# A causal attention step and a routed layer on one core: dense groups behind the last pair, transposes a pair ahead, x1 of the seventh step taken sooner

## The chip, the cores and the metric

The kernel runs on one core of a Trainium2 chip, as one launch. The core has TensorE (matmuls), VectorE, ScalarE, GpSimd and SyncE, which run their own instruction lists beside each other and wait for each other through semaphores. The metric is device time in microseconds (us). Traces are of one profiled execution; times in it count from the span's start.

## The reference

Two sequences of 2048 rows with 256 columns pass through two layers. The first: rows are normalized, three small networks (matmul, exact gelu, matmul) make q, k and v, masked scores without softmax weigh v, and the result, normalized again, is added to x. The second: each row is normalized and multiplied by one of 8 weight matrices, chosen by its position in the sequence.

```python
q, k, v = mlp_q(ln(x)), mlp_k(ln(x)), mlp_v(ln(x))     # gelu(x @ W1 + b1) @ W2 + b2
scores = einsum('bid,bjd->bij', q, k) / scale * tril
x = x + ln(einsum('bij,bjd->bid', scores, v)) * ln_w + ln_b
idx = argmax(pe @ sign(tile_sigs).T, axis=-1)          # one of 8 per position
y_all = einsum('bsd,tod->bsto', ln(x), W) + b
x = x + take_along_axis(y_all, idx, axis=2)
```

## The kernel before

**Numbers.** Float32 values are split in a rounded part and a rest, and a product is three matmuls (rounded by rounded, rounded by rest, rest by rounded; `mm3`, L493). Making an operand therefore takes two steps: ScalarE casts from PSUM ("rounded"), and VectorE subtracts the cast from the original ("rest").

**Attention.** The 4096 rows are taken in 8 steps of 512 rows, each of 4 chunks of 128. A state (k transposed times v) carries earlier steps. In the last step (s = LAST = 7) the chunks are handled by `last_scores`, `last_state` and `last_out`: output c of that step is its chunk c's attention result. GpSimd takes the powers for the two normalizations (`rstd_out`, `rstd_x1`), VectorE makes x1, the first layer's result (`x1_final`, `x1_stats`, `x1_var`).

**Sorting.** Rows of x1 go out by `rows_sorted`: an indirect DMA from GpSimd, one per chunk, which scatters them by their matrix into a buffer in HBM (`sorted_rows`), so that each slot of 128 rows needs one matrix. There are 37 slots; SyncE loads them back (`load_slot`). The last two chunks of the last step are not sorted ("dense", "unsorted"): all 8 matrices are applied to them and a one-hot factor picks the right result. Slots from 17 on may hold rows of step s = 6, the seventh, so their loads wait for its scatters; slots from 21 on wait for those of the last step's first two chunks.

**Pairs.** Slot 0 goes alone; the other 36 are 18 pairs, m = 0 to 17. A pair passes through: `pair_norm` (ScalarE, two instructions), `pair_transposes` (TensorE, 4 transposes), `pair_rounded` (ScalarE), `pair_rest` (VectorE), `pair_products` (TensorE, 12 matmuls), `pair_out` (VectorE adds the result to the rows) and two scatters to the output by GpSimd (`slots`). The 256 dense rows pass through the same places between pairs 11 and 12 (`PAIRS` stands for them). For that, `place` shifts the later pairs:

```python
        def place(m):
            return m if m < LATER else LATER if m == PAIRS else m + 1
```

`pair_transposes` takes a place and `pair_products` a pair; LATER is 12, so `pair_transposes(13)` turns the rows of pair 12. Products go to one bank, w_ps, for m < 8 and in turn to three from there; the transposes of places 5 to 7 share one bank (ring 1), and from 8 on there are three.

**Dense groups.** `dense_products(e, g)` is one of 8 groups of 6 matmuls with 512 columns (chunk e of the two, matrices 2g and 2g + 1), with two PSUM banks in turn; `dense_out` reads each with two VectorE instructions. When all four groups of a chunk are in, SyncE sends the chunk out.

**Order.** There is no scheduler: each engine's order is written out by hand in the blocks for the engines, and an engine that waits holds everything behind it in its list.

Of the kernel before, what the change touches and what calls it, by code (L numbers as in the profile page):

```python
# [37 lines left out]
CH = GT // P  # L38
PER = T // GT
STEPS = NB * PER  # L40
LAST = STEPS - 1
NT = 8
# [10 lines left out]
SLOTS = NB * NJ - DENSE + NT - 1  # L53
# [3 lines left out]
AMID, INNER, MIDDLE, LATER = 1, 5, 8, 12  # L57
# [15 lines left out]
def mk_seq_kernel(nc, x, w1, w2, bias_cols, rows3, sigs2, ffn_w, ffn_b, pe, out):  # L73
# [5 lines left out]
    with ExitStack() as ctx:  # L79
# [408 lines left out]
        def _(te):  # L488
# [193 lines left out]
            def dense_products(e, g):  # L682

                i = NT // 2 * e + g
                if i == 0:
                    te.wait_ge(xb_lo, AMID + LATER + 1)
                if i < 2:
                    te.wait_ge(o_cen, CH * STEPS)
                else:
                    te.wait_ge(dense_done, 2 * (i - 1))  # L690
                mm3(o_ps[i % 2][:, :], [[pair_xb(PAIRS, a)[:, cols(2 * e + k)] for a in range(2)] for k in range(KC)],
                    [[wf[:, a, k, 2 * g * C:2 * g * C + 2 * C] for a in range(2)] for k in range(KC)]
                    ).then_inc(dense_ps, 1)
# [17 lines left out]
            def last_state(c):  # L711

                if c == 0:
                    te.wait_ge(s_lo, splits_before(LAST, 0))
                i = CH * LAST + c
                if c < 2:
                    te.wait_ge(o_sq, i - 1)
                elif c == 3:
                    te.wait_ge(o_cen, i - 2)
                mm3(last_o[c][:, 0:C], [q_chunk(k, c) for k in range(KC)],  # L720
                    [[state[:, a, k * C:k * C + C] for a in range(2)] for k in range(KC)], stop=False)

            def last_out(c):
                if c == 0:
                    te.wait_ge(v_lo, 2 * STEPS)
                    te.wait_ge(off_lo, 3)
                    te.wait_ge(sc_lo, STEPS)
                pairs = []
                for j in range(c):
                    at = off_at[j] + (c - j - 1) * P  # L730
                    pairs.append([sc_off[:, a, at:at + P] for a in range(2)])
                pairs.append([scT[:, a, cols(c)] for a in range(2)])
                mm3(last_o[c][:, 0:C], pairs, [[vtok[:, a, j, :] for a in range(2)] for j in range(c + 1)], start=False
                    ).then_inc(o_ready, 1)
# [113 lines left out]
            pair_transposes(5)  # L848
            last_out(0)
            last_out(1)  # L850
            last_state(2)
            last_out(2)
            pair_products(5)
            last_state(3)
            last_out(3)
            pair_transposes(6)
            pair_products(6)
            pair_transposes(7)
            pair_products(7)
            pair_transposes(8)  # L860
            pair_products(8)
            pair_transposes(9)
            pair_products(9)
            pair_transposes(10)
            pair_transposes(11)
# [2 lines left out]
            pair_products(11)  # L868
            for m in range(LATER, PAIRS):
                pair_transposes(m + 1)  # L870
                dense_products((m - LATER) // 4, (m - LATER) % 4)
                pair_products(m)
            for i in range(PAIRS - LATER, NT):
                dense_products(i // 4, i % 4)

        @block.scalar
        def _(act):
# [218 lines left out]
            k_rounded(LAST, 0)  # L1096
            k_rounded(LAST, 1)
            pair_norm(4)
            v_rounded(LAST, 0)
            pair_rounded(4)  # L1100
            v_rounded(LAST, 1)
            last_rounded(1)
            last_rounded(0)
# [23 lines left out]
        def _(dve):  # L1127
# [447 lines left out]
            out_centred(s, 3)  # L1575
            pair_out(1)
            pair_rest(2)
            q_rest(LAST)
            pair_out(2)
            pair_rest(3)  # L1580
            x1_final(s, range(CH))
            k_rest(LAST, 0)
            x1_stats(s, range(CH))
            k_rest(LAST, 1)
            x1_var(s, range(CH))
            state_rest(s, 3)
            pair_out(3)
            v_biased(LAST, 0)
            pair_rest(4)
            v_biased(LAST, 1)  # L1590

            last_masked(1)
# [12 lines left out]
            out_centred(LAST, 1)  # L1605
            last_aggregates((0, 1))
            last_centred((0, 1))
            out_centred(LAST, 2)
            x1_final(LAST, (0, 1))
            x1_stats(LAST, (0, 1))  # L1610
            x1_var(LAST, (0, 1))
            pair_out(5)
            pair_rest(6)
            out_centred(LAST, 3)
            last_aggregates((2, 3))
            last_centred((2, 3))
# [14 lines left out]
            pair_out(11)  # L1631
            for m in range(LATER, PAIRS):
                pair_rest(m)
                g = m - LATER
                dense_out(g // 4, g % 4 * 2)
                dense_out(g // 4, g % 4 * 2 + 1)
                pair_out(m)
            for g in range(PAIRS - LATER, NT):
                dense_out(g // 4, g % 4 * 2)
                dense_out(g // 4, g % 4 * 2 + 1)  # L1640

        @block.gpsimd
        def _(pool):
# [167 lines left out]
            rstd_out(s)  # L1811
            slots((3, 4, 5, 6))
            rstd_x1(s)
            rows_sorted(s, (0, 1))
            slots((7, 8))
            pool.wait_ge(o_ready, CH * LAST + 2)
            rows_sorted(s, (2, 3))
            rstd_out(LAST, (0, 1))
            slots((9, 10))
            rstd_x1(LAST, (0, 1))  # L1820
            rows_sorted(LAST, (0, 1))
            rstd_out(LAST, (2, 3))
            slots((11, 12))
            rstd_x1(LAST, (2, 3))
            slots(range(13, SLOTS))


def position_table(seq, dim):
# [50 lines left out]
```

## Time and profile before

| | us |
|---|---|
| median of 3 runs | 312.46 |
| the runs | 312.4, 312.46, 314.71 |
| profiled execution, its time | 314.41 |
| profiled execution, its span | 312.7 |
| TensorE busy in the span | 288.1 |
| VectorE, ScalarE, GpSimd busy | 237.3, 188.3, 176.7 |

The span runs from the first to the last instruction in the profile; the execution's time is a little longer than it. The busy times are sums over the whole span. Mean granted TensorE clock over the span is 0.992 of full speed.

### The profile page before, as it was taken

The page shows a single profiled execution, that of the slowest core. Times are in us where ns is not written, and L with a number is a line of the kernel's source. Part 1 is how long each engine was busy: PE and PEld are TensorE (multiplying, and loading weights), DVE is VectorE, ACT ScalarE, POOL GpSimd, SP SyncE. Part 2 cuts the span into 40 slices and gives each one's busy share as a digit, 9 for nine tenths or more (in the row PEclk, how much of TensorE's full clock was granted, in tenths as well). Part 3 has the DMA queues.
Part 4 walks back from the last instruction along what each step waited for, and adds up shares of the span by engine and source line. Part 5 has one row for each costly group of instructions (what it writes and reads, how often), then busy time and mean ns, then how long its engine had stood idle before and what let it go on. Part 6 is the DMA issues. An engine that isn't in the chain of part 4 may idle for free.

```text
span 312.7 us, 5456 instructions
## 1 busy us (share of the span) xinstructions
PE 288.1 (92%) x1806; PEld 253.4 (81%) x1806; DVE 237.3 (76%) x539; ACT 188.3 (60%) x380; POOL 176.7 (57%) x238
## 2 busy tenths in 40 slices
PE   8999998998999999999999999999999985579991
PEld 6789887997888889889788989898988884477870
DVE  5769788899879978967995896788558778246661
ACT  2565775776656876786678658669674434264410
POOL 6881532360685568475737545584564578745452
PEclk9999999999999999999999999999999999979998
DMA  7909950011022120211031000260223234922110
GB/s 223 230 17 334 350 175 28 0 45 58 0 74 67 36 71 2 68 69 39 6 131 53 18 2 2 72 198 2 88 86 123 71 100 149 313 85 68 48 42 17
DMA packets 24209, 27.83 MB, mean 89 GB/s; under 512 B 4659, under 2 KB 22068, under 8 KB 24118
## 3 DMA queue, kind: packets, MB, share of 16 engines
q1 hardware_dynamic: 15910, 13.68, 14.7%
q0 software_dynamic: 3296, 8.64, 8.0%
q10 hardware_dynamic: 4976, 5.16, 4.9%
q8 instruction: 15, 0.25, 0.3%
q14 instruction: 12, 0.10, 0.1%
HBM read 13.95 MB, written 14.44 MB: 91 GB/s over the span
## 4 chain that ended last, share of the span: by engine, by line
PE 75%; DVE 13%; issue 5%; POOL 3%; ACT 2%; DVEq 0%; POOLq 0%; ACTq 0%
PE ring L493 40%; PE o_ps L493 11%; PE s_ps L493 6%; PE w_ps L493 3%; PE ring L502 2%; PE ring L521 2%; PE sc_ps L606 2%; DVE xres L1245 1%; POOL sorted_rows L1715 1%; PE sc_ps L604 1%; PE ring L764 1%; PE sc_ps L764 1%; DVE xnT L1166 1%; DVE st L1252 1%; DVE state L1210 1%
## 5 line engine op out<-in xcount | busy, mean ns | idle before, releaser
L493 PE MATMUL ring<-xnT,w_sp 128*128 128x512 f32 x288 | 73.5, 399 | 3.6 <-DVE hT L1171 1.7
L493 PEld LDWEIGHTS ring<-xnT,w_sp 128*128 128x128 f32 x288 | 51.9, 189 | 15.9 <-issue 3.3
L892 ACT ACTIVATE ring<-ring,b_cols 128x512 f32<-128x512 f32 x48 | 31.7, 660 | 27.1 <-PE ring L493 25.7
L493 PE MATMUL ring<-hT,w_sp 128*128 128x512 f32 x192 | 46.7, 397 | 0.2 <-DVE hT L1171 0.2
L1171 DVE TENSOR_TENSOR hT<-ring,hT 128x512 fp32r<-128x512 f32 x48 | 32.5, 681 | 13.8 <-ACT hT L895 12.2
L493 PEld LDWEIGHTS ring<-hT,w_sp 128*128 128x128 f32 x192 | 35.2, 188 | 8.8 <-DVE hT L1171 0.9
L1715 POOL DMA_INDIRECT sorted_rows<-xres,slot_i x30 | 31.3, 1042 | 12.3 <-issue 6.2
L1681 POOL TENSOR_TENSOR vtok<-v,vtok 128x512 fp32r<-128x512 f32 x14 | 18.0, 1286 | 25.0 <-ACT vtok L912 24.9
L1780 POOL DMA_INDIRECT out_dram<-slot_rows x22 | 21.8, 989 | 14.7 <-DVE slot_rows L1464 9.2
L895 ACT CAST hT<-ring 128x512 fp32r<-128x512 f32 x48 | 28.2, 587 | 1.5
L493 PE MATMUL s_ps<-vtok,ktok 128*128 128x256 f32 x168 | 24.8, 284 | 0.0
L1245 DVE SCALAR_TENSOR_TENSOR xres<-cen,rs,xres 128x256 f32<-128x256 f32 x32 | 23.7, 754 | 1.3 <-issue 1.0
L493 PEld LDWEIGHTS ring<-w_sp,hT 128*128 128x128 f32 x192 | 23.4, 188 | 0.7
L493 PE MATMUL ring<-w_sp,hT 128*128 128x256 f32 x192 | 23.9, 280 | 0.0
L493 PE MATMUL o_ps<-state,q_eye 128*128 128x256 f32 x116 | 23.2, 293 | 0.0
L1660 POOL TENSOR_SCALAR nm<-mv 128x4 f32<-128x4 f32 x7 | 1.6, 229 | 38.0 <-DVE mv L1160 38.0
L493 PEld LDWEIGHTS s_ps<-vtok,ktok 128*128 128x128 f32 x168 | 22.1, 191 | 0.0
L1674 POOL TENSOR_TENSOR xres<-xt,row_stage 128x1024 f32<-128x1024 f32 x8 | 22.0, 2752 | 0.0
L1780 POOL DMA_INDIRECT out_dram<-h x15 | 15.4, 1030 | 10.1 <-DVE h L1464 6.9
L1210 DVE TENSOR_TENSOR state<-s_ps,state 128x512 fp32r<-128x512 f32 x27 | 18.3, 678 | 2.1 <-ACT state L928 1.9
L945 ACT ACTIVATE xn<-xt,sh,rs 128x256 f32<-128x256 f32 x28 | 16.7, 598 | 4.9 <-POOL sh L1665 4.9
L493 PEld LDWEIGHTS o_ps<-state,q_eye 128*128 128x128 f32 x116 | 18.4, 190 | 1.5 <-issue 0.6
(241 smaller groups left out, 680.6 us busy)
## 6 DMA issues: line engine op xcount, KB each, us to landing
sorted_rows<-blank ACTq DMA_DIRECT2D x1, 5032.0 KB, 20.7
xt<-x SPq DMA_DIRECT2D x7, 512.0 KB, 3.5
slot_rows<-sorted_rows SPq DMA_DIRECT2D x22, 136.0 KB
w_stage<-tile_w SPq DMA_DIRECT2D x8, 256.0 KB, 3.2
h<-sorted_rows SPq DMA_DIRECT2D x15, 136.0 KB
xt<-x SPq DMA_DIRECT2D x2, 256.0 KB, 2.9
hT<-position_table POOLq DMA_DIRECT2D x1, 512.0 KB, 10.0
sorted_rows<-xres,slot_i POOLq DMA_INDIRECT x30
```

The lines of the kernel that those rows point to most:

```text
L493: last = te.matmul(o, lhs[k][a], rhs[k][c], start=start and k == 0 and i == 0, stop=stop and k == n - 1 and i == 2, skip_group_check=check)
L502: te.matmul(ring[2][:, :], warm_r[:, 0:P], warm_r[:, :], start=True, stop=True)
L892: nc.scalar.activation(full, ring[(2 + m) % 3][:, :], ACT.Gelu, bias=b1c[:, m // 2, m % 2:m % 2 + 1]).then_inc(gelu, 1)
L895: nc.scalar.copy(hT[:, m, 0, :], full).then_inc(h_hi, 1)
L945: last = nc.scalar.activation(xn[:, c, :], xt[s % 2][:, c, :], ACT.Identity, bias=sh1[:, c:c + 1], scale=rs1[:, c:c + 1])
L1171: nc.vector.tensor_tensor(hT[:, m, 1, :], ring[(2 + m) % 3][:, :], hT[:, m, 0, :].bitcast(F32), ALU.subtract).then_inc(h_lo_dve, 1)
L1210: nc.vector.tensor_tensor(state[:, 1, :], s_ps[:, :], state[:, 0, :].bitcast(F32), ALU.subtract).then_inc(s_lo, 1)
L1245: nc.vector.scalar_tensor_tensor(out=xres[s % XR][:, c, 0:C], in0=cen[:, c, :], scalar=rs2[:, c:c + 1], in1=xres[s % XR][:, c, 0:C], op0=A ...
L1674: nc.gpsimd.tensor_tensor(xres[s % XR][:, :, 0:C], xt[s % 2][:, :, :], lnb_row[:, :].unsqueeze(1).broadcast_to([P, CH, C]), ALU.add).then_ ...
L1681: nc.gpsimd.tensor_tensor(vtok[:, 1, 2 * j:2 * j + 2, :], v32[:, 2 * j:2 * j + 2, :], vtok[:, 0, 2 * j:2 * j + 2, :].bitcast(F32), ALU.sub ...
L1715: pool.indirect_dma_start(out=sorted_rows, out_offset=bass.IndirectOffsetOnAxis(ap=at, axis=0), in_=xres[s % XR][:, c, :], in_offset=None) ...
L1780: pool.indirect_dma_start(out=out_rows, out_offset=bass.IndirectOffsetOnAxis(ap=row_buf(n)[:, PLACE:PLACE + 1].bitcast(I32), axis=0), in_= ...
```

## The change

It moves work; nothing is computed differently. The matmuls are the same, and so are the DMAs.

- TensorE: the transposes of pairs 6 to 9 each stand one pair earlier, ahead of the products of the pair before. The transposes of pair 6 and the products of pair 5 stand ahead of state product and output 2 instead of behind them. In the loop over pairs 12 to 17 the dense group between transposes and products is gone; all 8 dense groups stand behind pair 17.
- ScalarE: the cast of pair 4 stands ahead of the first cast of v.
- VectorE: x1 of step s = 6 is made in two halves around q's rests, and its statistics and variance stand earlier; the rest of pair 4 stands ahead of both v additions. The addition of pair 5 and the rest of pair 6 stand ahead of x1 of the last step's chunks 0 and 1, and the statistics of output 2 behind it. The dense instructions stand behind pair 17.
- GpSimd: the four row scatters of step s = 6 go out in one piece, without a wait for output 1 of the last step; two more output scatters (slots 9 and 10) stand ahead of the first power of the last step, and the later slots move up accordingly.

```diff
@@ tensor
             last_out(0)
             last_out(1)
+            pair_transposes(6)
+            pair_products(5)
             last_state(2)
             last_out(2)
-            pair_products(5)
             last_state(3)
             last_out(3)
-            pair_transposes(6)
+            pair_transposes(7)
             pair_products(6)
-            pair_transposes(7)
+            pair_transposes(8)
             pair_products(7)
-            pair_transposes(8)
+            pair_transposes(9)
             pair_products(8)
-            pair_transposes(9)
             pair_products(9)
             pair_transposes(10)
             pair_transposes(11)
...
             for m in range(LATER, PAIRS):
                 pair_transposes(m + 1)
-                dense_products((m - LATER) // 4, (m - LATER) % 4)
                 pair_products(m)
-            for i in range(PAIRS - LATER, NT):
+            for i in range(NT):
                 dense_products(i // 4, i % 4)
@@ scalar
             pair_norm(4)
+            pair_rounded(4)
             v_rounded(LAST, 0)
-            pair_rounded(4)
@@ vector
             pair_rest(2)
-            q_rest(LAST)
+            x1_final(s, (0, 1))
+            q_rest(LAST, (0,))
+            x1_final(s, (2, 3))
+            q_rest(LAST, (1,))
             pair_out(2)
+            x1_stats(s, range(CH))
             pair_rest(3)
-            x1_final(s, range(CH))
+            x1_var(s, range(CH))
             k_rest(LAST, 0)
-            x1_stats(s, range(CH))
             k_rest(LAST, 1)
-            x1_var(s, range(CH))
             state_rest(s, 3)
             pair_out(3)
+            pair_rest(4)
             v_biased(LAST, 0)
-            pair_rest(4)
             v_biased(LAST, 1)
...
-            out_centred(LAST, 2)
+            pair_out(5)
+            pair_rest(6)
             x1_final(LAST, (0, 1))
             x1_stats(LAST, (0, 1))
             x1_var(LAST, (0, 1))
-            pair_out(5)
-            pair_rest(6)
+            out_centred(LAST, 2)
             out_centred(LAST, 3)
...
             for m in range(LATER, PAIRS):
                 pair_rest(m)
-                g = m - LATER
-                dense_out(g // 4, g % 4 * 2)
-                dense_out(g // 4, g % 4 * 2 + 1)
                 pair_out(m)
-            for g in range(PAIRS - LATER, NT):
+            for g in range(NT):
                 dense_out(g // 4, g % 4 * 2)
                 dense_out(g // 4, g % 4 * 2 + 1)
@@ gpsimd
             rstd_x1(s)
-            rows_sorted(s, (0, 1))
-            slots((7, 8))
-            pool.wait_ge(o_ready, CH * LAST + 2)
-            rows_sorted(s, (2, 3))
+            rows_sorted(s, range(CH))
+            pool.wait_ge(scores, CH * LAST + 2)
+            slots((7, 8, 9, 10))
             rstd_out(LAST, (0, 1))
-            slots((9, 10))
+            slots((11, 12))
```

On TensorE, in the turn of pair 17: the transposes (L764), then in before a dense group, then the first of the products (`ISA` rows set the address of the matrix).

```order
 L493 MATMUL s_ps<-wf,xnT 128x256 x2
 L764 MATMUL sc_ps<-ident,xn 128x128 x4
-L493 MATMUL o_ps<-wf,kT 128x512 x6
 L493 ISA
 L493 MATMUL ring<-wf,xnT 128x256
```

The group of 6 matmuls is taken out; the transposes and products of pair 17 stand directly behind each other. The end of TensorE's list:

```order
 L493 ISA
 L493 MATMUL ring<-wf,xnT 128x256 x2
-L493 MATMUL o_ps<-wf,kT 128x512 x12
+L493 MATMUL o_ps<-wf,kT 128x512 x48
 L79 UNCONDITIONAL_BRANCH
```

Behind pair 17 there were two dense groups (12 matmuls), and now there are eight (48).

On VectorE, where x1 of the last step's first two chunks is made (L1245), with its statistics (L1252) and variance (L1263), before:

```order
L1223 BN_STATS st<-s_ps 128x6 [waits o_ready]
L1245 SCALAR_TENSOR_TENSOR xres<-cen,rs,xres 128x256 [waits res_done,rstd2,o_cen]
L1245 SCALAR_TENSOR_TENSOR xres<-cen,rs,xres 128x256
L1252 BN_STATS st<-xres 128x6 [waits x1_made]
L1252 BN_STATS st<-xres 128x6
L1263 BN_AGGR mv<-st 128x2 [waits stat3,shift3]
L1263 BN_AGGR mv<-st 128x2
L1267 TENSOR_SCALAR nm<-mv 128x2 [waits aggr3]
L1268 TENSOR_SCALAR ve<-mv 128x2
L1464 TENSOR_TENSOR slot_rows<-w_ps,slot_rows 128x2x256 [waits y_ps]
L1456 TENSOR_TENSOR xb<-ring,xb 128x512 [waits xb_hi]
L1223 BN_STATS st<-o_ps 128x6 [waits o_ready]
```

and the same place changed (the lines are one lower there):

```order
L1463 TENSOR_TENSOR slot_rows<-w_ps,slot_rows 128x2x256 [waits y_ps]
L1455 TENSOR_TENSOR xb<-ring,xb 128x512 [waits xb_hi]
L1244 SCALAR_TENSOR_TENSOR xres<-cen,rs,xres 128x256 [waits res_done,rstd2,o_cen]
L1244 SCALAR_TENSOR_TENSOR xres<-cen,rs,xres 128x256
L1251 BN_STATS st<-xres 128x6 [waits x1_made]
L1251 BN_STATS st<-xres 128x6
L1262 BN_AGGR mv<-st 128x2 [waits stat3,shift3]
L1262 BN_AGGR mv<-st 128x2
L1266 TENSOR_SCALAR nm<-mv 128x2 [waits aggr3]
L1267 TENSOR_SCALAR ve<-mv 128x2
L1222 BN_STATS st<-s_ps 128x6 [waits o_ready]
L1222 BN_STATS st<-o_ps 128x6 [waits o_ready]
```

The addition of pair 5 and the rest of pair 6 (L1464 and L1456 in before) have moved ahead of x1, and the statistics of output 2 (`st<-s_ps`) behind it.

On GpSimd, from the row scatters of step s = 6 to the first power of the last step, before:

```order
L1715 DMA sorted_rows<-xres,slot_i 4736x272 [waits shift3]
L1715 DMA sorted_rows<-xres,slot_i 4736x272
L1780 DMA out_dram<-h 4096x256 [waits y_done] x2
L1715 DMA sorted_rows<-xres,slot_i 4736x272 [waits shift3,o_ready]
L1715 DMA sorted_rows<-xres,slot_i 4736x272
L1693 TENSOR_TENSOR ve<-mv,eps 128x2 [waits o_aggr]
L1695 TENSOR_TENSOR rs<-ve,half 128x2 [waits var2]
L1780 DMA out_dram<-h 4096x256 [waits y_done] x2
```

and changed (the lines are two lower there):

```order
L1713 DMA sorted_rows<-xres,slot_i 4736x272 [waits shift3]
L1713 DMA sorted_rows<-xres,slot_i 4736x272 x3
L1778 DMA out_dram<-h 4096x256 [waits y_done,scores]
L1778 DMA out_dram<-h 4096x256 [waits y_done] x3
L1691 TENSOR_TENSOR ve<-mv,eps 128x2 [waits o_aggr]
L1693 TENSOR_TENSOR rs<-ve,half 128x2 [waits var2]
L1778 DMA out_dram<-slot_rows 4096x256 [waits y_done] x2
```

The four row scatters stand together, their wait for output 1 (`o_ready`) is gone, and slots 9 and 10 stand ahead of the power.

## Rows read from the trace of the kernel before

**Rows 1.** The page: busy time, share of the span, instructions
```profile
PE 288.1 (92%) x1806; PEld 253.4 (81%) x1806; DVE 237.3 (76%) x539; ACT 188.3 (60%) x380; POOL 176.7 (57%) x238
```

**Rows 2.** Windows: busy us (instructions) in each stretch, clock, DMA share, GB/s
```profile
256.35:271.60 15.25, 9.14 (x70) 7.97 (x68) 9.71 (x27) 6.28 (x12) 12.03 (x16) 1.00 0.72 228
271.60:275.29 3.69, 0.00 (x0) 0.00 (x0) 0.98 (x2) 1.57 (x3) 2.90 (x3) 1.00 0.76 242
276.70:280.10 3.40, 3.40 (x18) 3.34 (x17) 1.98 (x3) 2.19 (x5) 0.54 (x1) 0.50 0.11 39
286.80:301.33 14.53, 14.21 (x89) 11.75 (x89) 9.22 (x17) 5.43 (x11) 7.49 (x9) 1.00 0.14 47
```

**Rows 3.** The chain that ended last: start us, us, what
```profile
297.71 1.70 PE s_ps L493 x12
299.41 0.44 PE sc_ps L764 x4
299.85 1.40 PE o_ps L493 x6
301.25 0.08 issue
...
303.04 2.82 PE o_ps L493 x12
```

**Rows 4.** Timeline of TensorE: start us, us, what, xcount [idle before <-releaser]
```profile
236.83 1.58 PE L493 MATMUL w_ps<-wf,xb 128*128 x12
...
243.72 0.50 PE L493 MATMUL sc_ps<-q_eye,kT 128*128 128x512 f32 x1 [0.46 <-DVE xb L1456]
...
258.43 1.69 PE L493 MATMUL w_ps<-wf,xb 128*128 x12 [1.48 <-DVE xb L1456]
259.96 0.60 PE L764 MATMUL ring<-ident,xn 128*128 128x128 f32 x4
262.04 1.70 PE L493 MATMUL w_ps<-wf,xb 128*128 x12 [1.48 <-DVE xb L1456]
...
265.84 1.70 PE L493 MATMUL ring<-wf,xnT 128*128 x12 [1.66 <-DVE xnT L1456]
...
271.00 0.60 PE L764 MATMUL ring<-ident,xn 128*128 128x128 f32 x4
```

**Rows 5.** Timeline of ScalarE
```profile
250.09 0.59 ACT L1013 CAST xb<-ring 128x512 fp32r<-128x512 f32 x1 [1.93 <-PE ring L764]
250.57 1.09 ACT L986 ACTIVATE xn<-slot_rows 128x255 f32<-128x255 f32 x2
...
260.59 0.58 ACT L1013 CAST xb<-ring 128x512 fp32r<-128x512 f32 x1 [2.04 <-PE ring L764]
...
273.67 0.58 ACT L1013 CAST xb<-ring 128x512 fp32r<-128x512 f32 x1 [4.08 <-remote]
```

**Rows 6.** Timeline of VectorE
```profile
254.75 0.88 DVE L1245 SCALAR_TENSOR_TENSOR xres<-cen,rs,xres 128x256 f32<-128x256 f32 x2 [1.04 <-issue]
...
262.18 0.88 DVE L1245 SCALAR_TENSOR_TENSOR xres<-cen,rs,xres 128x256 f32<-128x256 f32 x2 [0.28 <-POOL rs L1695]
...
264.42 0.68 DVE L1464 TENSOR_TENSOR slot_rows<-w_ps,slot_rows 128x512 f32<-128x512 f32 x1
265.02 0.68 DVE L1456 TENSOR_TENSOR xnT<-ring,xnT 128x512 fp32r<-128x512 f32 x1
267.58 0.69 DVE L1464 TENSOR_TENSOR slot_rows<-ring,slot_rows 128x512 f32<-128x512 f32 x1 [1.88 <-issue]
```

**Rows 7.** Timeline of GpSimd
```profile
251.40 0.96 POOL L1715 DMA_INDIRECT sorted_rows<-xres,slot_i  x1 [4.09 <-PE o_ps L493]
...
257.43 0.76 POOL L1704 TENSOR_TENSOR xres<-ve,half 128x2 f32<-128x2 f32 x1
...
261.36 0.72 POOL L1695 TENSOR_TENSOR rs<-ve,half 128x2 f32<-128x2 f32 x1
```

**Rows 8.** Timeline of SyncE's DMA queue
```profile
255.19 1.76 SPq L456 DMA_DIRECT2D slot_rows<-sorted_rows  x4
```

More of the change, by code:

```diff
@@ L1822, in _ @@
             rstd_out(LAST, (2, 3))
-            slots((11, 12))
+            slots((13, 14))
             rstd_x1(LAST, (2, 3))
-            slots(range(13, SLOTS))
+            slots(range(15, SLOTS))
 def position_table(seq, dim):
```

## The prediction

> **What bounds the kernel now.** I read the page first, then the end by stretches of time, then the chain of waits there, then each engine's timeline. The page says that TensorE is busy for 92% of the span and the others for 57 to 76% [rows 1]. That is an average. By stretches [rows 2], TensorE is busy from 256.35 to 271.60 us for 9.14 of 15.25 us; for the next 3.69 us it does nothing; from 286.80 to 301.33 us it is busy for 14.21 of 14.53 us. So two kinds of pair loop follow each other. In the first, TensorE waits in each turn; in the second, the wait is filled.
>
> The chain shows what fills it [rows 3]. One turn of the second loop is the products of a pair (1.70 us), the transposes of the next pair (0.44), one dense group (1.40) and a wait of 0.08: 3.62 us. The pair's other way, from the transposes through ScalarE's cast ("R" below) and VectorE's subtraction ("rest" below) to the products, runs beside the dense group and ends 0.08 us behind it. The first loop has no dense group, and its turn is as long: products start at 258.43, 262.04 and 265.84 us, 3.61 and 3.80 us apart, each after a wait of 1.48 to 1.66 us for VectorE [rows 4]. The turn there is the serial way itself: transposes to R 0.63 us (259.96 to 260.59), R to products 1.45 (to 262.04), products to the next transposes 1.53 (258.43 to 259.96), in sum 3.61 [rows 4, 5]. So a dense group costs TensorE nothing where it stands now.
>
> **The dense groups behind pair 17 (the largest term).** In before, six of the eight dense groups stand in the turns of pairs 12 to 17 and two behind pair 17. Changed, all eight stand behind it. The turns of pairs 12 to 17 still begin with the transposes of their own pair: behind LATER the place of pair m is m + 1, so `pair_transposes(m + 1)` turns the rows of pair m, and only the taken-out group stood between those transposes and the products that need them. So the turn keeps its serial length, 3.6 us as in [rows 4], and saves nothing. Behind pair 17 the six groups lie on the path in full: two of them back to back take 2.82 us of the chain [rows 3], 1.41 each, and 6 x 1.41 = **8.46 us**. VectorE doesn't stretch this: in the second loop it is busy for 9.22 of 14.53 us [rows 2], 2.30 a turn, and an addition and a rest of 0.69 each leave 0.92 for its two instructions of a group, less than 1.41, with two o_ps banks to go round. Bounds: if each turn shrank by the 0.08 us of waiting, 0.5 less; if the five whole turns came out like the slowest of the first loop, 3.80, 5 x 0.18 = 0.9 more. I take 8.46.
>
> **Transposes a pair ahead, pairs 6 to 9.** Here the change does put the next pair's transposes before the products, and R and the next rows' normalization run under them. What is left in a turn is products to VectorE's addition (265.84 to 267.58: 1.74), addition to rest (264.42 to 265.02: 0.60) and rest to products (265.02 to 265.84: 0.82) [rows 4, 6], since VectorE still takes the addition of pair m before the rest of pair m + 1. That is 3.16 us where 3.61 was, 0.45 a turn and not the whole wait of 1.48. Only pair 9 gets it clean: pair 8 is set by VectorE's statistics of the last step (next part), and from pair 10 on the order of the transposes is as before. Gain **0.45**.
>
> **VectorE and GpSimd ahead of pair 8.** I follow the changed order from where it first helps. TensorE waits 0.46 us at 243.72 for the rest of pair 4 [rows 4], whose R stood behind a v cast and whose rest stood behind a v addition. Both now go first, well before 243. TensorE goes on without the wait, so output 1, on which GpSimd's scatter at 251.40 waited in before [rows 7], is ready about 0.5 us sooner.
> The transposes of pair 6 now stand directly behind output 1. Their normalization comes from R of pair 5, 250.09 - 0.5, and ends 1.57 us later (250.09 to 251.66) [rows 5]: 251.2. TensorE waits some 0.6 us there, which the change adds; queued behind it on TensorE are the products of pair 5, outputs 2 and 3. VectorE waits for the first of these and takes outputs 2 and 3 later than before. Products of pair 5 then start at 251.5, and those of pair 6, with outputs 2 and 3 between, near 257.2 instead of 258.43.
> On VectorE the addition of pair 5 starts at 251.5 + 1.74 = 253.2, the rest of pair 6 at 253.8, the first two x1 chunks of the last step at 254.4 where they were at 254.75. From there to the end of their statistics and variance it is 2.3 us (262.18 to 264.42 and a little, for the same instructions) [rows 6]: 256.7 instead of 257.1. GpSimd took that variance only at 257.43, when its scatter before it was over [rows 7]. Now its two scatters there start with the addition of pair 5, 253.2 + 0.7, take 2 x 1.3 us and end at 256.5, so it takes the variance at 256.75, 0.7 us sooner, and with it the two row scatters and the power behind them (start 261.36). VectorE's last x1 chunks wait for exactly that power, by 0.28 us [rows 6]. So they, their statistics, the addition of pair 7, the rest of pair 8 and its products all come 0.7 us sooner: 265.84 becomes 265.1. That is **0.7 us** of gain. Bounds: 1.2 (TensorE's lead at pair 6 kept in full) and a loss of 0.6 (GpSimd a scatter of 1.3 us late).
>
> **x1 of the seventh step sooner.** Two additions of 0.44 us each (as at 254.75 [rows 6]) go in front of each half of q's rest, and statistics in front of the rest of pair 3, which comes some 0.7 us later, near 236.1. TensorE takes it at 236.83 [rows 4]; q's rest is first asked for later still. So this costs nothing while TensorE's queue covers it, and without that cover 0.7 us. GpSimd's four scatters of these rows go out together before 245 us; in before the last two waited for output 1 until 251.40 [rows 7]. SyncE's loads of slots 17 to 20, at 255.19 in before [rows 8], follow at about 246. But pair 8, their first user, was not waiting for them: it ran straight behind R of pair 7 (260.59) [rows 5]. I cost this at 0. The loads from slot 21 on hang on the last step's scatters, which come 0.7 us sooner; pair 10, their first user, comes 1.15 us sooner, behind work of some 4 us since they landed. GpSimd's scatters of a pair, 2 x 1.27 us, stay under the turn of 3.16 and cost nothing.
>
> **The sum.** -0.7 - 0.45 + 8.46 = **+7.3 us**. The profiled execution took 314.41 us for a span of 312.7; the median is 312.46. I take the difference as one event: the transposes of pair 10 start at 271.00 and R follows at 273.67, 2.0 us later than the usual 0.63 [rows 4, 5], with nothing of the program between. 314.41 - 2.0 = 312.4, the median. So the sum goes on the median: 312.46 + 7.3 = **319.8 us**. If the event comes in most executions of the changed kernel, 321.8. After the idle 3.69 us the granted clock is 0.50, the 1.2 GHz level, from 276.70 to 280.10, with TensorE busy all the while [rows 2]: that costs at most half of it, 1.7 us. I leave it where it is in both; without it in the changed kernel, 318.1.
>
> **The rivals.** (a) *The clock falls in the pair loop.* TensorE now rests some 1.5 us in each turn from 256 to 297 us, over 40 us where it was 15. Against it: through 15.25 us of the same rhythm the granted clock was 1.00 [rows 2]. For it: the fall at 276.70 came behind such turns and one longer pause. Price: at half the clock the products and transposes of a turn, 2.14 us, would take up to 2.1 more, 1.3 to 1.9 after what pipelining hides; 8 to 11 us in six turns: 328 to 331. Chance 7%. [...]
> (b) *The pair loop speeds up* (the case that is not slower). If the transposes of pairs 12 to 17 came a pair ahead of their products, a turn would be TensorE's own 1.70 + 0.44 and little else, 2.2 instead of 3.62: 6 x 1.42 = 8.5 back, and the result 311.3, within 1%. It decides from a turn of about 2.9 us down (8.46 - 1.15 - 3.1 = 4.2 us to win back in six turns, 0.7 each). Against it: the first loop, with the same order, turns in 3.61 [rows 4]. 3%.
> (c) *More is won in front.* SyncE's loads and GpSimd's scatters ran together up to 275 us at 228 to 242 GB/s [rows 2]. With four loads and two scatters moved ahead of that stretch, the late R at 273.67, the idle 3.69 us and the clock's fall could shrink in every execution. That gives up to 3 us: 317 to 318. 12%.
>
> **How the numbers follow.** Forecast 78%, (c) 12, (a) 7, (b) 3. Predicted 319.8. The range takes in the bounds of the loop (-0.5, +0.9), of the front (-0.5, +1.3), the event (+2.0) and most of (c): 317.5 to 323.0; outside lie (a), (b) and a part of (c). About 1%, 3 us, is what a measurement of this kernel can tell from no change. Slower by over 1%: 96%; within 1%: 3%; faster: 1%.
>
> **What would show it.** In the changed profile: turns of pairs 12 to 17 of 3.6 us, each with a wait of about 1.5 us for VectorE; eight dense groups in one run of some 11.3 us at the end; products of pair 9 some 3.2 us after pair 8's, and pair 8's at 265.1; the four scatters of step seven before 245 us and the load of slot 17 near 246; granted clock 1.00 through the loop. I am wrong if a turn of the late loop is under 3 us, if the clock falls inside it, or if pair 8 starts later than 265.8.

## The result, and the profile after

The changed kernel takes **318.8 us** (median of 4 runs, 316.95 to 320.04) beside 312.65 us for the kernel before on the same chip: ratio **1.0171, interval 1.0135 to 1.0208**. A second measurement on another chip (below) gave 318.85 beside 313.19, ratio 1.0151 [1.0117, 1.0185]. So it is slower, by 6.2 us in the first and 5.7 in the second, where 7.3 were forecast. The profiled execution took 316.95 us for a span of 315.2, at a mean granted clock of 0.994, and was the shortest of the four; the others had 0.973 to 0.983.

The page of the changed kernel: busy time, then TensorE's busy share and its granted clock in 40 equal slices of the span, in tenths:

```profile
PE 288.2 (91%) x1806; PEld 253.7 (80%) x1806; DVE 237.6 (75%) x539; ACT 189.0 (60%) x380; POOL 176.7 (56%) x238
...
PE   8999999998999999999999999999999984665695
...
PEclk9999999999999999999999999999999999899999
```

TensorE's row has the sixes of the pair loop, where it used to be full, and the nine of the dense groups behind it. The timeline of TensorE in the changed kernel (start us, us, what, then in brackets the idle time ahead and what ended it), from the first changed place to the end; it answers to [rows 4]:

```profile
236.20 1.58 PE L493 MATMUL w_ps<-wf,xb 128*128 x12
...
242.46 0.39 PE L493 MATMUL sc_ps<-q_eye,kT 128*128 128x512 f32 x1
...
250.34 0.66 PE L764 MATMUL ring<-ident,xn 128*128 128x128 f32 x4 [0.60 <-ACT xn L985]
250.76 1.69 PE L493 MATMUL w_ps<-wf,xb 128*128 x12
...
256.59 1.68 PE L493 MATMUL w_ps<-wf,xb 128*128 x12
...
264.85 1.70 PE L493 MATMUL ring<-wf,xnT 128*128 x12 [2.99 <-DVE xnT L1455]
268.01 1.71 PE L493 MATMUL w_ps<-wf,xnT 128*128 x12 [1.46 <-issue]
269.55 0.60 PE L764 MATMUL ring<-ident,xn 128*128 128x128 f32 x4
272.77 0.66 PE L764 MATMUL ring<-ident,xn 128*128 128x128 f32 x4 [2.62 <-ACT xn L985]
...
287.93 1.71 PE L493 MATMUL ring<-wf,xb 128*128 x12 [1.48 <-DVE xb L1455]
...
291.55 1.70 PE L493 MATMUL w_ps<-wf,xb 128*128 x12 [1.48 <-DVE xb L1455]
...
298.81 1.70 PE L493 MATMUL ring<-wf,xnT 128*128 x12 [1.48 <-DVE xnT L1455]
300.35 11.59 PE L493 MATMUL o_ps<-wf,kT 128*128 128x512 f32 x48
```

From pair 14 on the turns of the late loop are 3.62 us (287.93 to 291.55) with a wait of 1.48 in each (pair 13, ahead of them, waits 1.79), and the eight dense groups take 11.6 us in one run. Both are as forecast, and at first sight the sum of them explains the result. It doesn't: from the start of pair 17's products the changed kernel needs 315.2 - 298.8 = 16.4 us, and the kernel before needed 312.7 - 301.33 = 11.4 [rows 2]. That is 5.0 us more, not 8.46. Where the missing 3.5 us are shows in a view that the prediction did not open, GpSimd's timeline at the very end. The kernel before:

```profile
304.56 0.97 POOL L1780 DMA_INDIRECT out_dram<-h  x1 [1.38 <-DVE h L1464]
305.83 0.97 POOL L1780 DMA_INDIRECT out_dram<-h  x1 [0.30 <-issue]
```

and the changed one:

```profile
302.03 0.97 POOL L1778 DMA_INDIRECT out_dram<-h  x1 [1.37 <-DVE h L1463]
303.31 0.97 POOL L1778 DMA_INDIRECT out_dram<-h  x1 [0.30 <-issue]
```

In before, the span ends 6.9 us after GpSimd's last scatter began (305.83 to 312.7), and TensorE's last dense group was over by 305.9. SyncE's waits in the last microseconds of the kernel before (engine, line, what it waited for: us in total, times, longest):

```profile
SPq L79 <- PEq L79: 3.7, 1, 3.7
SPq L79 <- DMA out_dram<-xres: 0.7, 1, 0.7
SPq L485 <- DMA out_dram<-h: 0.6, 1, 0.6
```

and of the changed kernel:

```profile
SPq L79 <- DMA out_dram<-xres: 1.3, 1, 1.3
SPq L79 <- PEq L79: 0.2, 1, 0.2
```

Line 79 is the closing of the program, where the engines meet. In before, SyncE had seen the last scattered rows land (the wait at L485) and its own output too, and then stood there for 3.7 us; in the changed kernel for 0.2. The engine named is TensorE's queue, but TensorE had been done for long: the name only says that the one who came last is not seen. The experiments say who it was.

### The profile page after: what moved, and what is told of

Its sections match the earlier page's. It is cut to its first block, busy times and chain, and to the rows that moved or that the text cites. A ratio compares the mean times of both kernels' runs of the same rounds, so it can differ in the third digit from the quotient of the medians.

```text
span 315.2 us, 5456 instructions
## 1 busy us (share of the span) xinstructions
PE 288.2 (91%) x1806; PEld 253.7 (80%) x1806; DVE 237.6 (75%) x539; ACT 189.0 (60%) x380; POOL 176.7 (56%) x238
## 4 chain that ended last, share of the span: by engine, by line
PE 76%; DVE 11%; issue 6%; ACT 4%; POOL 1%; ACTq 0%; POOLq 0%; DVEq 0%
PE ring L493 41%; PE o_ps L493 11%; PE s_ps L493 6%; PE w_ps L493 3%; ACT xn L985 2%; PE ring L502 2%; PE ring L521 2%; PE sc_ps L606 2%; PE ring L764 1%; PE sc_ps L764 1%; PE sc_ps L604 1%; DVE xnT L1165 1%; DVE st L1151 1%; DVE xres L1244 1%; DVE xnT L1455 1%
```

## The experiments

All medians are device microseconds; the kernel before was run beside each: 313.01 us on the first chip (the first four kernels), 313.19 on the second (the next four), 313.16 on the third (the last four).

**1. Only the dense groups behind pair 17**, the rest as before.

```diff
             for m in range(LATER, PAIRS):
                 pair_transposes(m + 1)
-                dense_products((m - LATER) // 4, (m - LATER) % 4)
                 pair_products(m)
-            for i in range(PAIRS - LATER, NT):
+            for i in range(NT):
                 dense_products(i // 4, i % 4)
```

(and VectorE's two dense instructions of each group likewise)

> Only the dense groups are moved behind pair 17; all else as in the kernel before. My theory (the groups were hidden beside the serial way of a pair, and lie open behind pair 17): 6 x 1.41 = 8.5 us slower than before, 321.1; turns of pairs 12 to 17 of 3.6 us. Rival, the turn shrinks when the group is gone: 0 to 1 us slower. Rival, the granted clock falls in the loop in most executions: 1 to 3 us more, 322 to 324, and a mean clock near 0.975 in those runs.

Measured: 317.66 us, ratio 1.0159 [1.0126, 1.0193]: 4.7 us more than before, where the theory wanted 8.5. Its profiled execution had a granted clock of 1.00 throughout, turns of 3.62 us and 11.59 us of dense groups at the end. So the rhythm of TensorE is as forecast and the bill is 3.8 us short. The profiled span ends at 315.2, as the changed kernel's does.

**2. Only the front**: the changed kernel with the dense groups back in the loop, that is, the diff of run 1 taken the other way on the changed kernel.

> The changed kernel with the dense groups back in the turns of pairs 12 to 17, so the front edits alone. My theory: 1.15 us faster than before (0.7 in front of pair 8, 0.45 from pair 9), 311.5. Rival (c), the front edits also shrink the pause at pair 10: 2 to 4 us faster, 308.5 to 310.5. Rival, the front edits win nothing (TensorE's new wait at pair 6 eats it): 312.6.

Measured: 311.79 us, ratio 0.9951 [0.993, 0.9973], 1.2 us faster than before. The front's part of the sum (0.45 + 0.7 = 1.15) lies inside the interval, which runs from 0.8 to 2.2 us.

**3. Transposes really a pair ahead in the late loop**, on the changed kernel.

```diff
+            pair_transposes(LATER + 1)
             for m in range(LATER, PAIRS):
-                pair_transposes(m + 1)
+                if m + 2 <= PAIRS:
+                    pair_transposes(m + 2)
                 pair_products(m)
```

> The changed kernel, but the transposes of pairs 13 to 17 really stand a pair ahead in the late loop too. My theory (the turn is the serial way; without the cast in it, 3.16 us by addition, rest and products): 5 turns x 0.45 = 2.3 us faster than the changed kernel, 316.5. If the turn were TensorE's own work, 2.2 us: 7 us faster, 312. If GpSimd's two scatters (2.54) set it: 5.4 us faster.

Measured: 315.05 us, ratio 1.0066 [1.0041, 1.0091]. TensorE in its late loop:

```profile
286.69 1.71 PE L493 MATMUL ring<-wf,xb 128*128 x12 [1.02 <-DVE xb L1457]
289.85 1.70 PE L493 MATMUL w_ps<-wf,xb 128*128 x12 [1.02 <-DVE xb L1457]
```

The turn is 3.16 us, the one that the prediction worked out for pairs 8 and 9, from VectorE's order (addition of pair m ahead of the rest of pair m + 1). Here it is worth some 2.6 us in the span (312.6 where the changed kernel has 315.2). In the medians the run lies 2.0 us over before, where the changed kernel lies 5.7 to 6.2 over it.

**4. Idle matmuls in the late turns**, on the changed kernel, to see whether TensorE's resting costs clock there.

```diff
                 pair_transposes(m + 1)
+                te.wait_ge(o_cen, CH * STEPS)
+                for _ in range(6):
+                    te.matmul(o_ps[m % 2][:, :], warm_r[:, 0:P], warm_r[:, :], start=True, stop=True)
                 pair_products(m)
```

> The changed kernel with six idle matmuls (ones, into the dense banks, read by nobody) in each turn of pairs 12 to 17 where the dense group was. If the granted clock falls in the loop in most executions and costs time: mean clock back to 0.99 and 1.5 to 2.5 us faster than the changed kernel, 316.5 to 317. If the clock is no cost there: the same as the changed kernel, 318.8, or up to 0.5 us slower (the 0.08 us wait of each turn).

Measured: 317.32 us, ratio 1.0141 [1.0113, 1.0169], 4.3 us over before. In its profile the granted clock is 1.00 through the late loop, and from pair 12's products to pair 17's it is 18.43 us (279.78 to 298.21), the same as in the profile above (280.38 to 298.81). Whether this is less than the changed kernel could only be said with that kernel run again, which came next.

**5. The changed kernel again**, beside three kernels for the end of the program.

> The changed kernel itself, to stand on the same chip beside the next three. Both theories expect the ratio measured before, 1.017, so 317.5 to 319 us. The theories of this call are about why six dense groups moved behind pair 17 cost 4.7 us and not 8.5. Theory END: the kernel before does not end with its dense groups. GpSimd's last indirect scatter (rows of pair 17) starts at 305.83 us and the span ends 6.9 us later, at 312.7, while the dense branch (last addition 306.94, then the output's DMA) would have ended at 309.1. So the first 3.6 us of dense work moved behind pair 17 are free. Theory FRONT: the groups cost 1.41 each from the first on, and the turns of the pair loop or the work ahead of pair 12 came out faster by 3.6 us.

Measured: 318.85 us, ratio 1.0151 [1.0117, 1.0185], 5.7 us over before in the medians. This time the profiled execution has a span of 317.2, 2.0 more than the one above, and it shows where they go. TensorE in the turns of pairs 13 to 15:

```profile
284.01 2.32 PE L493 MATMUL s_ps<-wf,xnT 128*128 x12 [1.80 <-DVE xnT L1455]
286.12 1.05 PE L764 MATMUL sc_ps<-ident,xn 128*128 128x128 f32 x4
288.66 2.92 PE L493 MATMUL ring<-wf,xb 128*128 x12 [1.48 <-DVE xb L1455]
...
293.58 1.70 PE L493 MATMUL w_ps<-wf,xb 128*128 x12 [1.48 <-DVE xb L1455]
297.20 1.69 PE L493 MATMUL s_ps<-wf,xnT 128*128 x12 [1.48 <-DVE xnT L1455]
```

and the same stretches as windows (length, busy us of TensorE, its weight loads, VectorE, ScalarE and GpSimd, granted clock, DMA share, GB/s):

```profile
284.01:288.66 4.65, 3.17 (x16) 2.77 (x17) 1.38 (x2) 1.56 (x4) 2.05 (x3) 0.58 0.07 22
288.66:293.58 4.92, 3.44 (x17) 3.21 (x17) 1.38 (x2) 1.57 (x4) 1.60 (x3) 0.70 0.12 38
293.58:297.20 3.62, 2.14 (x16) 1.90 (x17) 1.38 (x2) 1.57 (x4) 1.87 (x3) 1.00 0.06 18
```

TensorE was granted the 1.2 GHz level in parts of two turns of the late loop, after turns in which it had rested 1.5 to 1.8 us each. They took 4.65 and 4.92 us instead of 3.62: 2.3 us, which is what parts this execution (317.2) from the one shown above (315.2). The six executions had mean clocks of 0.971 to 0.989. Such a mean does not say where the clock was low: in this profile it was also 0.53 and 0.50 from 264.01 to 270.90, at pairs 8 and 9. With idle matmuls in these turns (run 4) the distance to before is 4.3 instead of 5.7 us. That points the same way; the two were not run on one chip, and the intervals of their ratios overlap.

**6. Two of the six groups behind pair 17**, the rest as before.

```diff
                 pair_transposes(m + 1)
-                dense_products((m - LATER) // 4, (m - LATER) % 4)
+                if m < LATER + 4:
+                    dense_products((m - LATER) // 4, (m - LATER) % 4)
                 pair_products(m)
-            for i in range(PAIRS - LATER, NT):
+            for i in range(4, NT):
```

> The kernel before, with only the dense groups of pairs 16 and 17 taken out of the loop and put behind pair 17 (four of them stand there instead of two). END: 2 x 1.41 = 2.8 us lies inside the 3.6 us that GpSimd's end covers, so no change, -0.2 to +0.3 us, and the span still ends 6.9 us after the last scatter's start. FRONT: +2.8 us.

Measured: 312.78 us, ratio 0.9986 [0.9963, 1.0009]. TensorE's end and GpSimd's last scatter in its profile, whose span is 310.3:

```profile
298.95 1.70 PE L493 MATMUL ring<-wf,xnT 128*128 x12 [1.48 <-DVE xnT L1457]
300.49 5.80 PE L493 MATMUL o_ps<-wf,kT 128*128 128x512 f32 x24
```

```profile
303.45 0.97 POOL L1782 DMA_INDIRECT out_dram<-h  x1 [0.30 <-issue]
```

Twice the dense work behind pair 17, and no time that can be told from nothing: 303.45 to 310.3 is the same 6.9 us.

**7. The kernel before without the last two scatters.** The rows of slots 35 and 36 are computed and not written.

```diff
-            slots(range(13, SLOTS))
+            slots(range(13, SLOTS - 2))
...
-            sp.wait_ge(sent[1], 16 * (SLOTS - REUSED))
+            sp.wait_ge(sent[1], 16 * (SLOTS - REUSED - 2))
```

> The kernel before without the two indirect scatters of pair 17's rows (slots 35 and 36 are computed and not written to the output; SyncE waits for two fewer). END: the last scatter left starts at about 302.2 in the profile of before, 3.6 us sooner, so GpSimd's end comes at 309.1 and meets the dense branch's 309.1: 3.3 to 3.6 us faster. FRONT: the dense groups set the end and nothing changes.

Measured: 310.31 us, ratio 0.9892 [0.9858, 0.9925], 2.9 us faster in the medians, 3.4 by the ratio. GpSimd's last scatter and SyncE's closing wait:

```profile
300.02 0.98 POOL L1780 DMA_INDIRECT out_dram<-h  x1 [0.30 <-issue]
```

```profile
SPq L79 <- DMA out_dram<-xres: 1.3, 1, 1.3
SPq L79 <- PEq L79: 0.2, 1, 0.2
```

TensorE's and VectorE's work is all there, the dense groups are where they were, and only GpSimd does less: the closing wait falls from 3.7 to 0.2 us. So what the end waited for hangs on GpSimd's last scatters. Whether it is the engine itself or its DMA queue the run can't tell, since both have less to do. The span is 306.9, again 6.9 us after the last scatter's start, and just there the dense way ends too.

**8. Transposes a pair ahead (run 3), and four dense groups back in the loop**, the four of pairs 12 to 15.

```diff
                 if m + 2 <= PAIRS:
                     pair_transposes(m + 2)
+                if m < LATER + 4:
+                    dense_products((m - LATER) // 4, (m - LATER) % 4)
                 pair_products(m)
-            for i in range(NT):
+            for i in range(4, NT):
```

> The changed kernel with the transposes of pairs 13 to 17 a pair ahead in the late loop (as in the run where that took turns of 3.16 us) and the dense groups of pairs 12 to 15 back in the loop, four left behind pair 17. END: four turns take TensorE's own 1.70 + 0.44 + 1.40 = 3.54, 0.38 more than 3.16, so pair 17 starts 1.5 us later than in that run (297.7), its last scatter at 302.2 and GpSimd's end at 309.1; the dense branch ends at 312.6 - 5.6 + 1.5 = 308.5. Span 309.1, so about 3.5 us less than the run without them and 2 to 2.5 us faster than before: near 310.8. FRONT: 309.0 to 310, since each group moved in gains 1.41 - 0.38.

Measured: 312.04 us, ratio 0.9949 [0.9924, 0.9973]; the expectation of END was 310.8. The end keeps to END's rule (last scatter 304.48, span 311.3), but all of it came later than expected: the products of pair 12 started at 283.92, where run 10 below, with the clock kept at 1.00, has 282.48. The granted clock from 264.39 to 283.92 was 0.65. The turns with a dense group took 3.28 us (TensorE has no wait in them), less than the 3.54 worked out and only 0.12 more than run 3's turns without one.

**9. VectorE takes the rest of pair m + 1 before the addition of pair m**, on run 8.

```diff
+            pair_rest(LATER)
             for m in range(LATER, PAIRS):
-                pair_rest(m)
+                if m + 1 < PAIRS:
+                    pair_rest(m + 1)
                 g = m - LATER
...
                 pair_out(m)
```

> The run with transposes a pair ahead and four dense groups in the loop (312.04 us), and VectorE takes the rest of pair m + 1 before the addition of pair m in the late loop. Where the serial way (products to addition 1.74, addition to rest 0.60 + 0.69, to products 0.13) sets the turn, it falls from 3.1 to what GpSimd's two scatters take, 2.54; the four turns with a dense group stay at TensorE's own 3.27. So the starts of pairs 16 and 17 gain 0.6 and 0.6: 1.1 to 1.2 us faster than 312.04, about 310.9. If TensorE's queue or GpSimd set those two turns already: no change, 312.0.

Measured: 310.56 us, ratio 0.9922 [0.9894, 0.995]: 1.5 us less than run 8 in the medians, expected 1.1 to 1.2. The two stood on different chips, and by the ratios to before the gain is 0.8 us, with intervals that overlap; the turns show it more plainly. The last turns of TensorE:

```profile
292.38 1.60 PE L493 MATMUL w_ps<-wf,xb 128*128 x12
293.81 0.60 PE L764 MATMUL sc_ps<-ident,xn 128*128 128x128 f32 x4
294.17 1.68 PE L493 MATMUL s_ps<-wf,xnT 128*128 x12
295.90 1.70 PE L493 MATMUL ring<-wf,xnT 128*128 x12
```

No wait is left: 1.79 and 1.73 us where run 8 had 3.07 and 3.15. What is left at the end is GpSimd, scatter behind scatter at 1.28 us from 296.78 to 301.90, and then its 6.8 us (span 308.7).

**10. Idle matmuls ahead of pairs 8 and 9 and of two transposes**, on run 8.

```diff
             pair_transposes(9)
+            te.wait_ge(o_cen, CH * STEPS)
+            for _ in range(11):
+                te.matmul(o_ps[1][:, :], warm_r[:, 0:P], warm_r[:, :], start=True, stop=True)
             pair_products(8)
```

(5 more ahead of the products of pair 9, 6 each ahead of the transposes of pairs 11 and 13)

> The run with transposes a pair ahead and four dense groups in the loop (312.04 us), plus idle matmuls (ones by ones into a free bank, nobody reads them) where TensorE waits: 11 ahead of the products of pair 8, 5 ahead of pair 9's, 6 ahead of the transposes of pair 11 and 6 ahead of those of pair 13. Theory CLOCK: the granted clock of 0.50 in pairs 8 to 12 (13.65 us of it in that profile, with pair 12 at 283.92 where it stood at 280.1 to 280.4 with 3.4 us of it) comes from TensorE's resting, and the idle matmuls keep it at 1.00: 1.5 to 2.5 us faster, near 310. Theory HARMLESS: the clock falls all the same or its cost lies beside the waits: 0 to 0.5 us slower, for the idle matmuls that overrun a wait.

Measured: 311.48 us, ratio 0.9942 [0.9918, 0.9965]. The clock is kept, 0.993 to 1.00 in all eight runs; the gain is 0.6 us in the medians and 0.2 by the ratios, inside the uncertainty, and not 1.5 to 2.5.

**11. Runs 9 and 10 together.**

> Both of the two runs above together. CLOCK and the shorter turns add up: 309 to 309.5 us, 1.1 to 1.3% faster than before, the fastest kernel here. HARMLESS: 310.9 to 311.4.

Measured: 310.28 us, ratio **0.9907 [0.9879, 0.9936]**, the fastest complete kernel of this study: 2.9 us faster than before and, by the ratios, 2.4% faster than the changed one. The idle matmuls are worth 0.3 us of it, which can't be told from nothing.

**12. Idle matmuls in the kernel before**, 6 each ahead of the products of pairs 8 and 9 and of the transposes of pair 11.

> The kernel before with 6 idle matmuls (1.4 us) ahead of the products of pair 8, of pair 9, and of the transposes of pair 11. In its profile TensorE rested 1.5 us in each of these turns, then 3.70 us ahead of pair 11's transposes, and ran at 0.50 from 276.70 to 280.10. CLOCK: no fall there, and pairs 10 and 11 take 1.7 instead of 2.1 to 2.4 us: 0.5 to 1.5 us faster than before. If the pause of 3.7 us has a cause of its own (not TensorE's rest), it stays, and the gain is under 0.5 us. HARMLESS: no change or 0.3 slower.

Measured: 315.6 us, ratio 1.008 [1.0053, 1.0107], 2.4 us slower: neither theory. TensorE's transposes of pairs 10 and 11:

```profile
270.37 0.60 PE L764 MATMUL ring<-ident,xn 128*128 128x128 f32 x4
270.73 1.64 PE L871 MATMUL o_ps<-warm_r 128*128 128x512 f32 x6
275.95 1.11 PE L764 MATMUL ring<-ident,xn 128*128 128x128 f32 x4 [3.59 <-ACT xn L993]
```

and VectorE's addition of pair 9, then ScalarE's R of pair 10:

```profile
272.89 0.69 DVE L1471 TENSOR_TENSOR slot_rows<-w_ps,slot_rows 128x512 f32<-128x512 f32 x1 [4.21 <-remote]
274.32 0.59 ACT L1020 CAST xb<-ring 128x512 fp32r<-128x512 f32 x1 [5.38 <-remote]
```

R (ScalarE's cast) comes 3.95 us after the transposes' start where 0.63 is usual [rows 4, 5], and the addition 4.07 after the start of its products (268.82) where 1.74 is usual. The pause is there though TensorE had been kept busy ahead of it, so TensorE's resting there isn't its cause. It is longer than in the profile of before (R 2.67 us after the transposes' start there), by 1.3 us; where the rest of the 2.4 us comes from is not shown.

## Why the prediction was right, and where its sum was not

The forecast was 319.8 us with a range of 317.5 to 323.0; 318.8 and 318.85 were measured. The sign and the range held, and so did the mechanism: the dense groups lay hidden in the late turns and lie open behind pair 17. The sum held less well: its largest term was 3.5 us too big, and most of that came back through a rival to which 7% had been given. That the total came within 1 us is luck in this part.

**The dense groups: the term that was mis-sized.** The prediction's step was "Behind pair 17 the six groups lie on the path in full". The work is there in full (11.59 us, where two groups took 2.97: 8.6 us for six, turns unchanged at 3.62 from pair 14 on, each with its 1.48 of waiting, as worked out). But the path did not end there. The prediction took the chain of waits for the end of the program; that chain closes with VectorE's last addition at 306.94, and the span with 312.7, and it never asked what lies between. Two ends race: the last dense addition's end plus 2.15 us for output 7 (313.05 to 315.2 in the changed kernel, 315.04 to 317.2 in run 5, 310.42 to 312.6 in run 3), and the last scatter's start plus 6.9 us. In before they stood at 309.1 and 312.7. So the first 3.6 us of dense work put behind pair 17 were free, and six groups cost 8.6 - 3.6 = 5.0 us (4.9 with the forecast's 8.46). Run 1 measured 4.7, run 6 measured nothing for two groups (2.8 us of work), and run 7 took GpSimd's last scatters away and found the other end some 3 us in front. So the failed term is settled; what fills the 5.9 us behind the last scatter's end is not.

**The front.** Run 2 measured 1.2 us for it alone, where 1.15 were forecast. Step by step against the profile after, which was already 0.5 us early ahead of the first changed place (pair 1's products at 226.33, 226.87 in before) and 0.6 at pair 3's products (236.20, 236.83 in [rows 4]): the wait for the rest of pair 4 is gone (242.46, no wait); the new wait at pair 6's transposes is 0.60 as said; products of pair 5 at 250.76 (251.5 forecast), of pair 6 at 256.59 (257.2), of pair 8 at 264.85 (265.1), of pair 9 3.16 us later (3.16). Taken from pair 3 on, pair 8 comes 0.4 us sooner, where 0.7 was forecast, and pair 9 0.5 more, where 0.45 was forecast.

**x1 of the seventh step at no cost.** It held: the only wait that TensorE shows from 236.20 on until the one at 250.34 is 0.34 us at the transposes of 238.12, and before has the same one (238.75). The rest of pair 3 started at 234.74, no later than in before (234.85), where the prediction had it near 236.1. The four row scatters started between 238.72 and 242.66, and the loads of slots 17 to 20 at 245.18 (near 246 forecast).

**The event at pair 10.** The prediction took 2.0 us off for it and said that the median had none. Here the runs disagree with it. In nine of the 14 profiles the transposes of pair 11 follow those of pair 10 after 3.2 us or more (4.29 in before, 3.22 in the changed kernel, 3.50, 3.22, 3.39 and 4.20 in runs 1, 2, 6 and 7; 3.21, 3.23 and 5.58 in runs 10, 11 and 12, which have idle matmuls between), where 2.26 is enough in run 3. So at least 1 us of it is in most profiles, and it varies by another 1 to 2. How often it comes in one kernel is not shown, with one or two profiles of each; the changed kernel has it in its first profile and not in run 5. The pause did shrink, as rival (c) has it, in the changed kernel's profile (2.62 us of idle time for 3.70), but run 1, without the changed front, had 2.90: the front didn't do it.

**The rivals.** (a), the clock falls in the pair loop, was given 7% and a price of 8 to 11 us for six turns. Its mechanism is real, in part: of the two profiles of the changed kernel one has the fall, in two turns of six, at 1.0 and 1.3 us a turn. That brings back 2 of the 3.5 us by which the main term was too big, and makes the total look right. The profile without the fall is of the fastest of the ten executions (316.95 us), so it seems to come in most of them, but no other execution has a profile; the slowest, 320.04 us, isn't explained. The Trainium skill, page TensorE: Matmul & The Clock Gate, section HAM oscillation — how this bites in real kernels, describes a loop in which each short burst of matmuls stands behind a wait for a transfer, longer than the burst, and runs at the low clock in every turn. Here the wait (1.48 us) is shorter than the work of a turn (2.14), and the low level came in two turns of run 5 (0.58 and 0.70) and in none of the first profile's loop, so this is not that section's case. (b), the loop speeds up, did not happen: the order is what the prediction read from the diff, and only the runs that move the late transposes (3 and 8 to 11) get shorter turns.

**What stays open.** In the medians the dense groups alone and the front alone add up to +3.4 us; together they gave +5.7. The fall of the clock is 2.0 to 2.3 us of that in the execution seen. Why the changed kernel has lower mean clocks than run 1 (0.971 to 0.994 in ten executions, against 0.983 to 1.00 in six), though the two loops are the same, isn't known. Nor is the cause of the pause at pair 10, or what it is that the program's end waits for behind the last scatter.

## What to carry to other kernels

Before costing work that is moved to the end of a program, list every engine's last instruction and the distance from there to the span's end; the chain of waits stops at the last instruction that it knows, and the difference between the two ends is what can be added for nothing. An engine that is idle in each turn is filled best with work of its own that is needed anyway: a dense group cost nothing in the loop as long as transposes and products stood serially, and 0.12 us once they didn't (run 8 beside run 3). When a total agrees with the forecast, check the terms all the same: here a term 3.5 us too big and a rival of 2 us partly cancelled each other.

## What the runs showed of the hardware

- This program, whose last GpSimd instruction is an indirect scatter, ends 6.8 to 6.9 us after that scatter's start, 5.9 after its end, if nothing else is later: 6.87 in before, 6.88, 6.85, 6.88, 6.82, 6.8, 6.8, 6.84 and 6.86 in runs 2, 6, 7, 8, 9, 10, 11 and 12. The last scattered rows had landed by then: SyncE's wait for them (0.6 us in before) lies ahead of the 3.7 us at the closing. Where dense work ended last, the span closed 2.15 us after VectorE's last addition.
- At half the granted clock a turn takes less than twice its time: a turn of the late loop with products at the 1.2 GHz level took 4.92 us for 3.62, since 1.5 us of it is waiting. In front the loss was given back by pair 11: run 3 had pair 8's products at the low level (2.92 us for 1.70), and its transposes of pair 11 started at 272.75, the changed kernel's, at the high level but with the pause, at 272.77.
- The pause at pair 10 is in all nine profiles whose granted clock had stayed at 1.00 through pairs 8 and 9, and in none of the five where it had fallen to about 0.50 there: from one set of transposes to the next 2.26, 2.50, 2.38, 2.71 and 2.69 us in runs 3, 4, 5, 8 and 9. That does not make the clock its cause. In those five the transposes of pair 10 start later, at 270.49 to 270.97 us, where seven of the nine have 269.28 to 269.85. ScalarE's cast behind them starts at about the same time in both: 271.13 to 272.03 in the five, 270.88 to 271.96 in those seven. So something may hold the cast until about then whatever the clock did. The transfers that run beside it are a rival that no run tested. In before the cast comes at 273.67, just as they thin out (mean share of the 16 DMA engines 0.99 from 271.00 to 273.50, 0.43 in the 2 us behind that), which speaks for it; in the changed kernel the cast comes at 271.15 with the share still at 1.05 from 271.00 to 272.00, which speaks against it. Whether TensorE's signal or its reader is late is not shown either; in run 12 both VectorE and ScalarE were late.
